# Spiking feed-forward layer: three groups in one step

## The reference

```python
h = jnp.square(jax.nn.relu(jnp.einsum('bsd,fd->bsf', x, W_fc)))
y = jnp.einsum('bsf,df->bsd', h, W_proj)
# five times, from mem = 0 (BETA = 0.9, THRESHOLD = 1.0):
reset = spike_fn(mem - THRESHOLD)             # 1.0 where mem > 1, otherwise 0.0
mem_new = BETA * mem + y - reset * THRESHOLD
# spike = spike_fn(mem_new - THRESHOLD); the layer gives the mean of the five spikes
x = _layernorm(x + mean_of_spikes, axis=-1)   # (v - mean) / sqrt(var + 1e-5)
```

## Time and profile before

| | us |
|---|---|
| median of 3 runs | 11147.57 (11145.72 to 11165.72) |
| the profiled execution | 11157.64, its span 11155.5 |
| TensorE busy | 8653.4 (78% of the span) |
| VectorE busy | 6076.7 (54%) |
| ScalarE busy | 4464.0 (40%) |
| mean granted TensorE clock | 0.843 |

### The profile page before, as it was taken

How to read it: one execution, slowest core, us unless ns; L and a number is a source line. 1 busy time by engine, 2 the same in 40 slices (tenths; PEclk the granted TensorE clock), 3 DMA queues, 4 the chain that set the end, 5 groups by cost and what they waited for, 6 DMA issues and landing times. The chain is left out here.

```text
span 11155.5 us, 122278 instructions
## 1 busy us (share of the span) xinstructions
PE 8653.4 (78%) x42558; PEld 4737.6 (42%) x42670; DVE 6076.7 (54%) x11571; ACT 4464.0 (40%) x7824; POOL 1932.4 (17%) x1926
## 2 busy tenths in 40 slices
PE   4887575957889798989878788788786899566665
PEld 1222253532333366456434344444343444345454
DVE  6777331026777365266239678755444565455553
ACT  3666131113555464155127456542111444233332
POOL 1100102020111011011001001100000100366666
PEclk8888667977999899999978789788776999778787
DMA  2321322112222000000000000000001322355556
GB/s 63 51 43 22 58 68 72 61 42 37 39 39 39 16 1 10 0 13 1 9 13 1 1 1 1 1 10 0 5 0 23 58 42 42 109 174 177 175 175 180
DMA packets 243487, 521.55 MB, mean 47 GB/s; under 512 B 55051, under 2 KB 94837, under 8 KB 241431
## 3 DMA queue, kind: packets, MB, share of 16 engines
q1 hardware_dynamic: 154887, 232.49, 10.4%
q0 software_dynamic: 88064, 282.15, 8.5%
HBM read 425.31 MB, written 75.53 MB: 45 GB/s over the span
## 5 line engine op out<-in xcount | busy, mean ns | idle before, releaser
L818 ACT ACTIVATE probs<-scores 128x1024 f32<-128x1024 f32 (+4 forms) x960 | 868.8, 937 | 892.7 <-PE scores L695 630.0
L907 DVE TENSOR_REDUCE row_max<-ring 128x1 f32<-128x512 f32 (+3 forms) x1792 | 1024.8, 625 | 246.9 <-PE ring L669 218.1
L3332 POOL DMA_INDIRECT r_got<-in_L_ffn_tables,r_pick_now x960 | 945.3, 985 | 424.4 <-issue 280.9
L695 PE MATMUL scores<-query_stack,key_stack 99*128 99x512 bf16 (+3 forms) x2816 | 850.9, 393 | 162.1 <-DVE levels L929 77.7
L3428 PE MATMUL r_psum_y<-r_diagonal,r_got 128*128 128x128 f32 x4096 | 648.7, 334 | 420.6 <-ACT r_diagonal L3475 420.6
L715 PE MATMUL outputs<-probs,head_values 128*32 128x512 f32 (+3 forms) x5632 | 781.2, 629 | 102.5 <-ACT probs L815 99.8
L3428 PEld LDWEIGHTS r_psum_y<-r_diagonal,r_got 128*128 128x128 f32 x4096 | 630.2, 247 | 489.0 <-ACT r_diagonal L3475 484.8
L815 ACT ACTIVATE probs<-levels,quant 128x1024 f32<-128x1024 uint8 x512 | 612.7, 1234 | 328.5 <-DVE levels L929 325.2
L929 DVE TENSOR_SCALAR levels<-scores 128x1024 uint8<-128x1024 f32 x512 | 607.4, 1219 | 178.4 <-PE scores L695 146.3
L669 PE MATMUL ring<-key_stack,query_stack 96*128 96x512 bf16 (+3 forms) x1792 | 608.7, 382 | 65.1 <-DMA key_stack<-normed_parts 41.2
L3253 DVE TENSOR_TENSOR_SCAN state<-decay,added 128x1024 f32<-128x1024 f32 x256 | 583.4, 2279 | 33.4 <-ACT decay L3227 33.0
(11 more groups left out here) (597 smaller groups left out, 15551.2 us busy)
## 6 DMA issues: line engine op xcount, KB each, us to landing
joined_heads<-heads_out SPq DMA_DIRECT2D x512, 32.0 KB, 2.0
expert_w<-in_L_ffn_w SPq DMA_DIRECT2D x16, 1024.0 KB, 10.8
r_got<-in_L_ffn_tables,r_pick_now POOLq DMA_INDIRECT x960, 3.7
quant_parts<-parts SPq DMA_DIRECT2D x48, 256.0 KB, 5.1
query_stack<-quant_parts SPq DMA_DIRECT2D x48, 256.0 KB, 8.6
key_stack<-quant_parts SPq DMA_DIRECT2D x48, 256.0 KB, 8.0
query_stack<-cross_parts SPq DMA_DIRECT2D x48, 256.0 KB, 8.3
normed_parts<-parts SPq DMA_DIRECT2D x48, 256.0 KB, 5.3
```

What stands on the lines that cost most here:

```text
L695: last = nc.tensor.matmul(out[:, off:GROUP], keys, q_stack[0:rows, h, half * GROUP + off:(half + 1) * GROUP], start=True, stop=not edge)
L818: nc.scalar.activation(dst, s_ps[0:k_rows, 2 * (e % 2):2 * (e % 2) + 2, off:GROUP], ACT.Exp, scale=scale).then_inc(probs_ready, 1)
L907: nc.vector.reduce_max(row_max[:, i, qt, at:at + 1], src[:, 0:cols], AX.X).then_inc(ring_read, 1)
L3332: nc.gpsimd.indirect_dma_start(out=b["got"][:, n, :], out_offset=None, in_=b["tables"], in_offset=bass.IndirectOffsetOnAxis(ap=b[picks][:, ...
```

## The change

The two steps of a turn become one, and the work is staggered over three groups: in one step group g − 2 is normalised (`closing`), group g − 1 has its spikes counted (`spiking`), and group g has its hidden and drive products computed (`driving`). `spiking_ffn` calls `spiking_step` with (None, None, 0), (None, 0, 1), six times in a loop with (g − 2, g − 1, g), then (6, 7, None) and (7, None, None). The normalisation no longer calls `add_norm`: its matmuls stand at fixed places among TensorE's products (mean after hidden chunk 2, variance after hidden chunk 6, spread after drive chunk 3), its ScalarE work behind the Squares of chunks 5 and 7, and its VectorE work ahead of the spike steps 0, 2 and 4 and at the end. There are four banks for the hidden products instead of two, and the drive products run over n outside and c inside. The multiply by 1/5 is folded into the addition of x. The last spike addition writes the total into a second buffer that the next step reads.

```diff
-        h_ps = ctx.enter_context(banks(nc, "hidden_psum", [P, 2, GROUP], F32))
-        y_ps = ctx.enter_context(banks(nc, "drive_psum", [P, FC, GROUP], F32))
-        norm_ps = ctx.enter_context(banks(nc, "norm_psum", [P, 4, GROUP], F32))
-        def group(now, following):
...
-                        for c in range(FC):
-                            for n in range(ic):
-                                pe.wait_ge(squared, n + 1)
-                                last = nc.tensor.matmul(y_ps[:, c, :], w2[:, n, c * P:(c + 1) * P], h[:, n, :], start=(n == 0), stop=(n == ic - 1))
...
-                        then(nc.vector.tensor_scalar(total[:, :, :], total[:, :, :], 1.0 / steps, None, ALU.mult))
-            if now is not None:
-                add_norm(chip, [group_slice(now)], norm_ps, ready=lambda _, c: total[:, c, :])
-
-        group(None, 0)
-        with nc.Fori(0, GROUPS - 1) as g:
-            group(g, g + 1)
-        group(GROUPS - 1, None)
+        with banks(nc, "hidden_psum", [P, 4, GROUP], F32) as h_ps, banks(nc, "drive_psum", [P, FC, GROUP], F32) as y_ps, banks(
+                nc, "norm_psum", [P, 2, GROUP], F32) as norm_ps:
+            b["h_ps"], b["y_ps"], b["mean_ps"], b["rstd_ps"] = h_ps, y_ps, norm_ps[:, 0, :], norm_ps[:, 1, :]
+            spiking_step(chip, b, None, None, 0)
+            spiking_step(chip, b, None, 0, 1)
+            with nc.Fori(2, GROUPS) as g:
+                spiking_step(chip, b, g - 2, g - 1, g)
+            spiking_step(chip, b, GROUPS - 2, GROUPS - 1, None)
+            spiking_step(chip, b, GROUPS - 1, None, None)
...
+            def drive_hidden(n):
+                if n >= 4:
+                    pe.wait_ge(relu_ready, n - 3)
...
+            def drive(n):
+                if n == 0 and spiking is not None:
+                    pe.wait_ge(y_taken, 1)
+                pe.wait_ge(squared, n + 1)
+                for c in range(FC):
+                    nc.tensor.matmul(y_ps[:, c, :], b["w2"][:, n, c * P:(c + 1) * P], h[:, n, :], start=(n == 0), stop=(n == ic - 1))
...
+            for n in range(ic):
+                if driving is not None:
+                    drive_hidden(n)
+                if closing is not None and n == 2:
+                    mean()
+                if closing is not None and n == 6:
+                    variance()
+            for n in range(ic):
+                if driving is not None:
+                    drive(n)
+                if closing is not None and n == 3:
+                    spread()
+
+        @block.scalar
+        def _(act):
+            for n in range(ic):
+                if driving is not None:
+                    act.wait_ge(h_ready, n + 1)
+                    nc.scalar.activation(h[:, n, :], h_ps[:, n % 4, :], ACT.Relu).then_inc(relu_ready, 1)
+                    act.wait_ge(relu_ready, n + 1)
+                    nc.scalar.activation(h[:, n, :], h[:, n, :], ACT.Square).then_inc(squared, 1)
+                if closing is not None and n == 5:
+                    for c in range(FC):
+                        act.wait_ge(centred, c + 1)
+                        nc.scalar.activation(sq[:, c, :], z[:, c, :], ACT.Square).then_inc(z_squared, 1)
+                if closing is not None and n == ic - 1:
+                    act.wait_ge(var_ready, 1)
+                    nc.scalar.activation(root, rstd_ps[:, 0:per], ACT.Sqrt, bias=chip.eps[:, 0:1]).then_inc(root_ready, 1)
...
+            def close_sum():
+                for c in range(FC):
+                    last = stt(out=z[:, c, :], in0=last_total[:, c, :], scalar=1.0 / SPIKE_STEPS, in1=x(c), op0=ALU.mult, op1=ALU.add)
+                    last.then_inc(summed, 1)
...
+            closes = {0: close_sum, 2: close_centre, 4: close_root} if closing is not None else {}
+            if spiking is not None:
+                copy(y, y_ps[:, :, :]).then_inc(y_taken, 1)
+            for s in range(SPIKE_STEPS):
+                if s in closes:
+                    closes[s]()
...
+                    if s == 1:
+                        if closing is not None:
+                            dve.wait_ge(summed, FC)
+                        then(copy(total, spike))
+                    then(ts(spike, mem, SPIKE_AT, None, ALU.is_gt))
+                    then(tt(last_total if s == SPIKE_STEPS - 1 else total, total, spike, ALU.add))
+            if closing is not None:
+                close_scale()
```

More of the change, by code:

```diff
@@ L1946, in spiking_ffn @@
     ic = inner // P
-    steps, beta, threshold = 5, 0.9, 1.0
     with ExitStack() as ctx:
         sb = lambda name, shape: ctx.enter_context(sbuf(nc, name, shape, F32))
[L1950 to L1953, removed]
-        h_ps = ctx.enter_context(banks(nc, "hidden_psum", [P, 2, GROUP], F32))
-        y_ps = ctx.enter_context(banks(nc, "drive_psum", [P, FC, GROUP], F32))
-        norm_ps = ctx.enter_context(banks(nc, "norm_psum", [P, 4, GROUP], F32))
-        def group(now, following):
[L1960 to L1963, removed]
-                        for n in range(ic):
-                            if n >= 2:
-                                pe.wait_ge(relu_ready, n - 1)
-                            for c in range(FC):
-                                last = nc.tensor.matmul(h_ps[:, n % 2, :], w1[:, c, n * P:(n + 1) * P], chip.xt[:, c, group_slice(following)],
-                                                        start=(c == 0), stop=(c == FC - 1))
-                            last.then_inc(h_ready, 1)
-                        if now is not None:
-                            pe.wait_ge(y_taken, 1)
-                        for c in range(FC):
-                            for n in range(ic):
-                                pe.wait_ge(squared, n + 1)
-                                last = nc.tensor.matmul(y_ps[:, c, :], w2[:, n, c * P:(c + 1) * P], h[:, n, :], start=(n == 0), stop=(n == ic - 1))
[L1977 to L2001, removed]
-                        then(nc.vector.tensor_scalar(total[:, :, :], total[:, :, :], 1.0 / steps, None, ALU.mult))
-            if now is not None:
-                add_norm(chip, [group_slice(now)], norm_ps, ready=lambda _, c: total[:, c, :])
-        group(None, 0)
-        with nc.Fori(0, GROUPS - 1) as g:
-            group(g, g + 1)
-        group(GROUPS - 1, None)
@@ new lines, in spiking_ffn @@
+        b = {"w1": sb("fc_w", [P, FC, inner]), "w2": sb("proj_w", [P, ic, DIM])}
+        b["h"] = sb("hidden", [P, ic, GROUP])
+        for name in ("drive", "membrane", "spike", "spikes_now", "spikes_last"):
+            b[name] = sb(name, [P, FC, GROUP])
+        load(nc, [(b["w1"][:, :, :], io["L2_ffn_w1"].rearrange("(c p) n -> p c n", p=P)), (b["w2"][:, :, :], io["L2_ffn_w2"].rearrange("(c p) n -> p c n", p=P))])
+        with banks(nc, "hidden_psum", [P, 4, GROUP], F32) as h_ps, banks(nc, "drive_psum", [P, FC, GROUP], F32) as y_ps, banks(
[7 more added lines that the diff above has]
+            spiking_step(chip, b, GROUPS - 1, None, None)
```

53 lines of the change are left out of this document (added).

## The result

The changed kernel takes 11058.28 us in the median of four runs (11035.53 to 11063.89) against 11146.65 before: the ratio is 0.9913, with a 95% interval from 0.9899 to 0.9927, that is 97 us less (81 to 113).

A forecast was written before the change was run, and what follows sets the result against it. The normalisation chain, bare for 15 us a turn, was to go, leaving TensorE as bound. Layer 374.8 to 310.0 us, 64.8 less; minus 10 for clock falls, gain 54.8: median 11147.57 to 11092.8 us, range 11070 to 11119.

The forecast's parts named there:

- The bound and the removed chain: In each loop turn: about 15 us of uncovered normalisation chain goes, and TensorE bounds the merged step, 34.9 us a turn.
- The new wait at the variance: In each merged step, TensorE waits 1.1 us before the variance for ScalarE's two squares of z.
- VectorE's waits and cover: In each merged step, VectorE waits 1.9 us for the root, then for the spread, and ends 5.4 us before TensorE.
- The boundary: Between steps, barrier, cleared semaphores and the loop's branch take 1.5 us.
- The banks: Rival: drive products alternating between two PSUM banks cost time, up to 110 us, kernel 55 slower; chance 0.04.
- The sum of the layer: Whole spiking layer: 31.4 + 28.75 + 6 × 34.9 + 25.8 + 14.7 = 310.0 us against 374.8, 64.8 less.
- clock term: In the six full turns: falls of TensorE's clock, 0.75 a step at 2.2 us each, cost 10 us.
- the two last steps: At the layer's end: closing group 6 with counting group 7 takes 25.8 us, the last bare chain 14.7.
- Other layers moving by more than some us, which nothing here would explain: Outside the changed layer: a sign that the prediction is wrong, with no chance given.

## Why the prediction was wrong

- **The bound and the removed chain: right.** The turn is bound by TensorE, at 34.4 us where 34.9 was laid out; the bare chain is gone; closing it without cover gives two thirds of the layer's gain back.
- **The new wait at the variance: right in kind, a little large.** 1.1 us expected, 0.67 idle measured. The two squares take 1.13 and not 1.26 (7602.21 to 7603.34), and TensorE comes to the variance 13.99 us after its first product (7588.73 to 7602.72), not 13.7.
- **VectorE's waits and cover: right.** 1.85 for the root against 1.9; 1.78 for the spread against 1.3; done 6.5 us ahead of the next copy, boundary included, against 5.4 before the boundary.
- **The boundary: right.** 1.33 to 1.39 against 1.5. In front of the written-out turn, which has no branch, it is 1.00, so the branch was worth 0.33.
- **The banks: right,** shown by the run with the old order.
- **The sum of the layer: its clock term failed, and other terms were a little large.** The sum said 310.0 before the clock. The trace has 307.9 with it, so 304.5 without: each turn is 34.4 us and not 34.9 (3.0 in six), and the two last steps take 38.1 us (7762.40 to 7800.50) where 25.8 + 14.7 = 40.5 was laid out. The term "6 × 0.75 × 2.2 = 10 us" was mis-sized twice. The number of falls was two in six turns, not 4.5: the stretch was 2.62 us and not 3.05, and falls don't grow evenly with length (none at 1.84, two at 2.62, six at 4.34). The boundaries caused none. And a fall costs 1.7, not 2.2. The term is 3.4 us. So of the 12.1 us that the layer's gain lay over the forecast (66.9 against 54.8), 6.6 are this term and 5.5 the others. Had I left the clock out altogether, the gain of 64.8 would have been 2.1 us from the layer's 66.9, but by luck: two errors that cancel.
- **"Other layers moving by more than some us, which nothing here would explain": this happened.** The step that failed is the unspoken one that the rest of the kernel keeps its time. Medians gained 88 us, the layer 66.9, so some 21 came from elsewhere, 26.7 behind the layer in the profiled pair. Of the 33.6 us by which the medians passed the forecast, that is 21.5, and the layer's 12.1 are the rest. The range allowed 13 for it, from the spread of three runs of one kernel. This is what carried the time out of the range. Even the right layer would have given 11079.7.
- **Where those 21 us come from stays open.** Shown is: they appear on chips of the first kind (gains of 97 and 100 us) and not on the second (69 and 61); 5 to 8 us of the stretch behind are one late transfer and a fall of the clock beside it, in every trace of the unedited before and of that size in no other; an edit of before that leaves the work alone moved it by 11 to 18 us; with one fixed set of semaphores in both kernels the difference is 68 us, about the layer's own. Argued only: that the numbering of later steps is the cause.

## A version that beats both

The variance one product later and one clear a step: 11019.54 us in the median against 11152.72 for before on the same chip, 0.9880 (0.9865 to 0.9895), 134 us less. The changed kernel has 0.9913 (0.9899 to 0.9927), on another chip. The late variance takes 8 us from the layer, without the fixed semaphores (307.9 to 300.0) and with them (306.1 to 298.4), which whole runs can hardly tell (0.9890 against 0.9880).

## What to carry to other kernels

A chain of short steps between engines that runs bare in each turn is worth most of its length if another group's dense work can be laid over it (here 9.3 us of about 15 a turn, 43.7 to 34.4, since its matmuls still take their time on the bounding engine); place each link a few us after the time when its input is ready, as here the mean and the spread, and look at each wait on the bounding engine, since 0.7 us too early cost 0.9 a turn and the clock as well. Forecast the changed stage by its sum, and give the range of the whole a term for stages that are not touched: the stage here repeats to 0.2 us and the whole kernel by no better than 20. Count what every step boundary does, clears too: one fixed run of semaphores took 55 us off the kernel before and some 24 off the changed one.

## What was not expected of the hardware

- One fixed run of semaphores for all steps, 310 clears fewer, took 55 us (38 to 71) off a kernel of 11150, though in the trace each extra clear takes 0.06; in the changed kernel 263 fewer took 22 to 26. Whether it is the clears or the numbering that does this is not shown.
- A transfer of a few rows, issued at the same place of the same code, landed after 6.7 to 7.9 us in the three traces of one kernel and after 1.8 to 5.5 in the 16 others, and TensorE waited up to 4.9 us for it.
- The granted clock fell in none of six turns with 1.84 us of one-column matmuls between dense products, in two with 0.67 us of idle time ahead of them, in six with 2.39. Each fall cost 1.7 us where dense products followed, one of them 3.4.
- The last layer, which gathers rows by indirect DMA, takes about 200 us longer on some chips than on others with the same kernel (behind the layer: 3268 to 3277 against 3476 for before).
